# In-degrees by scans over sorted runs, rows scaled by ScalarE, plain one-hots in the first pass of a graph kernel

## The chip, the cores and the metric

The kernel runs on one core of a Trainium2 chip. Its time is the device time of one launch in microseconds (us); lower is better. The kernel before has been timed in three runs, and one more execution was recorded by the profiler. All numbers of busy time and of single instructions come from that one profiled execution.

## The reference, cut to what matters

A graph of 6250 nodes with 256 features and 106,250 edges (source, target, weight). The edges are sorted by target: `dst = dst[argsort(dst)]`, and every node has at least its self-loop. Four graph layers follow one another, with a layer norm after each. Only the first has something to do with the change:

```python
deg_out = segment_sum(edge_weight, src, num_segments=N)
deg_in  = segment_sum(edge_weight, dst, num_segments=N)
norm    = edge_weight * rsqrt(deg_out[src] * deg_in[dst] + EPS)
# one layer: xt = x @ W ; agg = segment_sum(xt[src] * norm[:, None], dst) ; relu(agg + b)
```

This layer is applied twice with the same edges and norms (the first and the second pass below). A later layer divides by the number of edges that end in a node (the counts), and the last one sums over the edges in both directions.

## The kernel before, in words

The nodes are cut into 49 blocks of 128. The edges are laid out so that each *tile* of 128 edges has its targets in one block; the first pass has 888 tiles (`T`), later passes 880. A tile's messages are summed in three steps. GpSimd (POOL) gathers the 128 source rows from a table in HBM into a slot of a ring (one indirect DMA of 128 x 257 numbers: 256 features, and in column 257 the source's out-degree). TensorE (PE) multiplies the rows with a one-hot matrix, edge by node of the block, into one of four PSUM banks. VectorE (DVE) adds the bank to the block's sums in SBUF (`acc`).

**Preamble.** Edges are loaded as 128 partitions of 840 (`J`) edges, sorted. DVE plans the layout by target (`plan_by_dst`, `place_blocks`, L1646 to L1649). Edge records of three words (source, target, weight) go to HBM (L614), and POOL reads windows of them back (`windows`), which PE turns so that each tile is a column (`turn_windows`): `d_idx` (source row), `d_loc` (node of the block), `d_norm` (at first the weight). Out-degrees are sums of products of one-hots (`out_degrees`, DVE L1671 to L1674, PE L791), in chunks between the other steps. PE transposes the layers' weights (L825 to L835) behind the first chunks. Then come the in-degrees: in 74 batches of 12 tiles DVE makes bf16 one-hots of `d_loc` (L1682) and PE multiplies them with the weights split into three bf16 parts and a column of ones (L800), two tables of sums per tile are reduced (L1690, L1691) and summed by block on PE (L813). Meanwhile POOL waits for the out-degrees, which SyncE (SP) writes into the table (L406, L408), and then fills the ring of 40 slots (L660), ahead of the pass. `l0_ready` starts the pass on PE and ScalarE (ACT).

**First pass.** All engines run loops of 40 tiles (a *turn*: five *octets* of 8 tiles): 17 turns in which DVE also places ranks for a later pass, 5 without, and one last octet. The order of DVE is written out by hand in `scatter_turn`: for tile u it does the extras of `next_norms` or `with_places`, makes the one-hot of tile u times the norm (L1871, one scalar instruction: equal, then multiply), and adds tile u - 2 (L1860). The extras compute the norms of the next octet. SP loads the octet's target numbers, broadcast to all partitions (L418, 256 KB); at u = 0 of an octet DVE compares them with the node numbers (`row_onehots`, L1919); PE multiplies the result with the table of in-degrees (`degrees_of`, L917, eight bf16 matmuls) to give the in-degree of each edge; at u = 4 DVE reduces three parts (L1925) and multiplies with column 257 of the gathered rows (L1931); ACT takes the root (L1275); at u = 6 DVE inverts it (L1936) and multiplies it into `d_norm` (L1938). PE's loop is `first_pass` (L934, a matmul of 256 columns per tile). POOL's is `first_gathers`, which waits until the matmul that last read a slot is done. ACT also turns the gather's indices into integers for the next turn (L1271). At u = 2, 18, 34 of the first 17 turns DVE places one block of source ranks (`place_of_block`): compare 840 edges with the block (L1721), scan them (L1722), copy where the mask is set (L1724).

After the pass a dense stage, the second pass (its tables are read at L630) and the three further layers follow. The change doesn't touch them.

Of the kernel before, what the change touches and what calls it, by code (L numbers as in the profile page):

```python
# [99 lines left out]
def build(nc, A, out):  # L100
# [26 lines left out]
    ROW_BUF = (0, 1, 2, 0, 1)  # L127
# [17 lines left out]
    with ctx:  # L145
# [9 lines left out]
        numbers = bank[6][:, 0:P]  # L155

# [33 lines left out]
        parts_d = acc_flat[:, 10240:10240 + 2 * TC].bitcast(BF16).rearrange("p (t w) -> p t w", w=4)  # L190
        loc_k = acc_flat[:, 0:TC].bitcast(BF16).rearrange("p (t r) -> p t r", r=2)
# [30 lines left out]
        def part(n, dt=F32):  # L222
# [14 lines left out]
        mask = part(J // 2, BF16)  # L237
# [3 lines left out]
        ROWS = RING * P  # L241
        loc_rows, row_oh = (big[:, at_dst + o:at_dst + o + 3 * ROWS // 2].bitcast(BF16).rearrange("p (v n) -> p v n", v=3)
                            for o in (0, 3 * ROWS // 2))
        assert 3 * ROWS <= 7 * J // 2 + 2 * J
# [8 lines left out]
        w_sums, c_sums = s_idx[:, :], s_loc[:, :]  # L253
        loc_w = ring[:, TG * 512:TG * 512 + TG * P // 2].bitcast(BF16).rearrange("p (g n) -> p g n", g=TG)
# [9 lines left out]
        turned_sums = oh[:, 0:7, :].rearrange("p r n -> p (r n)")  # L264
# [59 lines left out]
        waited pool_waited act_waited first_staged totals_ready listed signs codes win_free acc_clear sums_ready sums_t sums_c sums_done sort_low sort_high sort_mm sort_out places table_in degrees locs_out locs_ready di_oh di_mm di_z root  # L324
        s_ready dego_mm dego_oh loc_ready prefix_done flag_ready win_d_ready diag_ready
        blk_bcast slow_pos rec_d_done win_d_in win_turned deg_oh
        deg_mm
# [38 lines left out]
        def _(sp):  # L366
# [35 lines left out]
            sp.wait_ge(S["locs_ready"], 1)  # L402
            sp.dma_start(loc_dram.rearrange("(g p n) -> p g n", p=P, n=P), loc_w).then_inc(S["locs_out"], 16)
# [5 lines left out]

            sp.wait_ge(S["locs_out"], 16)  # L410
            sp.wait_ge(S["codes"], 1)

            def load_rows(i, v, since):

                if since is not None:
                    sp.wait_ge(S["di_oh"], i * WIDE + (v - since + 1))
                b = ROW_BUF[v]
                sp.dma_start(loc_rows[:, b, :], loc_dram[ds(i * (WIDE * ROWS) + v * ROWS, ROWS)].partition_broadcast(P)).then_inc(rows_in[b], 16)  # L418

# [783 lines left out]
        def _(act):  # L1203
# [55 lines left out]
            for k, first in ((0, 0), (1, 3)):  # L1259
                if k:  # L1260
                    act.wait_ge(S["sums_done"], 1)
# [1198 lines left out]
```

## Time and profile before

| | us |
|---|---|
| median of three runs | 8519.04 (8510.78 to 8534.96) |
| profiled execution, its own time | 8506.99 |
| its span, first to last instruction | 8505.2 |
| busy in the span: PE / DVE / ACT / POOL | 5829.8 / 4220.0 / 1769.0 / 4359.4 |
| preamble (first one-hot of the pass at 401) | about 400 |
| last add of the first pass | 1813 |

Read the table so: the busy times overlap, and a share over the whole span says little about one stage. The preamble and the first pass are together 1813 us of 8505; DVE was busy in them 1203 us, POOL 912 us, PE 1090 us and ACT 161 us. The mean granted clock of PE over the span was 0.704 of full speed (2.4 GHz); in the first pass the windows of 200 us show 0.63 to 0.69.

### The profile page before, as it was taken

What the parts mean: (1) busy time and instruction counts of PE and PEld (TensorE: products, weight loads), DVE (VectorE), ACT (ScalarE), POOL (GpSimd) and SP (SyncE); (2) the same over time, 40 slices, a digit from 0 to 9 for tenths busy, and PEclk for the clock granted to TensorE, in tenths of its full rate; (3) what the DMA queues carried; (4) which work ended last, traced back from release to release, by engine and by line L of the source; (5) the groups of instructions that cost most, each with busy time, mean ns of one, the idle gap of its engine ahead of it and who ended that gap; (6) DMA issues with size and microseconds to landing.
All of it is one profiled execution on the core that took longest, in us unless ns stands there. A gap on an engine that the chain in (4) does not pass through costs nothing. (4 is left out here: it accounts for less than half of the span.)

```text
span 8505.2 us, 118243 instructions
## 1 busy us (share of the span) xinstructions
PE 5829.8 (69%) x23570; PEld 3830.4 (45%) x23571; DVE 4220.0 (50%) x10149; ACT 1769.0 (21%) x3207; POOL 4359.4 (51%) x4466
## 2 busy tenths in 40 slices
PE   5466666678888887996666666797666666666564
PEld 4333333345555555674454444454333333333332
DVE  8766666545555555884555555565222222222224
ACT  4100000015666663122222222253000000000000
POOL 0266666626666665004555555302666666666664
PEclk7566666689999998767878887897555555555555
DMA  2133333333222221232222222411221113111112
GB/s 81 41 103 99 100 99 100 106 91 102 81 81 82 81 81 50 78 131 87 72 72 73 73 72 72 95 33 42 56 56 50 45 45 45 45 45 46 44 45 63
DMA packets 309340, 609.28 MB, mean 72 GB/s; under 512 B 89530, under 2 KB 163590, under 8 KB 309064
## 3 DMA queue, kind: packets, MB, share of 16 engines
q0 software_dynamic: 184128, 466.71, 20.4%
q1 hardware_dynamic: 125064, 141.13, 5.5%
q14 instruction: 121, 0.99, 0.0%
q8 instruction: 27, 0.44, 0.0%
HBM read 563.79 MB, written 50.13 MB: 72 GB/s over the span
## 5 line engine op out<-in xcount | busy, mean ns | idle before, releaser
L895 PE MATMUL bank<-ring,oh 128*128 128x128 f32 x3520 | 1350.3, 495 | 960.3 <-DMA ring<-fwd_table,stage_i 465.4
L895 PEld LDWEIGHTS bank<-ring,oh 128*128 128x128 f32 x3520 | 876.1, 312 | 1556.2 <-issue 1552.2
L630 POOL DMA_INDIRECT ring<-h_table,stage_i x880 | 877.2, 997 | 658.4 <-issue 326.3
L1860 DVE TENSOR_TENSOR acc<-bank,acc 128x256 f32 x1768 | 749.9, 424 | 797.4 <-PE bank L974 389.7
L630 POOL DMA_INDIRECT ring<-fwd_table,stage_i x880 | 832.1, 946 | 508.5 <-issue 267.6
L630 POOL DMA_INDIRECT ring<-bwd_table,stage_i x880 | 832.4, 946 | 448.4 <-PE bank L895 221.5
L1321 ACT ACTIVATE ring<-big 128x889 f16<-128x889 f16 x840 | 831.3, 1032 | 539.0 <-PE bank L985 335.8
L985 PE MATMUL bank<-ring,big 128*128 128x445 f16 (+1 forms) x3360 | 826.6, 370 | 146.6 <-ACT ring L1321 123.2
L1110 PE MATMUL bank<-big,oht 128*128 x2640 | 457.1, 340 | 481.8 <-ACT oht L1436 461.9
L660 POOL DMA_INDIRECT big<-x_and_degree,stage_i x536 | 533.2, 995 | 447.5 <-PE bank L934 286.2
L934 PE MATMUL bank<-big,oh 128*128 128x256 f32 x1072 | 507.3, 620 | 356.5 <-DVE oh L1871 278.5
L1902 DVE TENSOR_TENSOR acc<-bank,acc 128x1024 f32 x220 | 269.3, 1224 | 920.0 <-PE bank L895 757.9
L1871 DVE TENSOR_SCALAR oh<-iota,d_loc,d_norm 128x128 f32<-128x128 f32 x1768 | 632.4, 361 | 102.5 <-issue 34.6
L974 PE MATMUL bank<-ring,oh 128*128 128x256 f32 x1760 | 576.1, 412 | 125.2 <-DVE oh L1871 92.0
L985 PEld LDWEIGHTS bank<-ring,big 128*128 128x128 f16 x3360 | 478.5, 146 | 379.1 <-ACT ring L1321 161.3
L1110 PEld LDWEIGHTS bank<-big,oht 128*128 128x128 bf16 x2640 | 306.2, 116 | 624.1 <-issue 531.3
L1126 PE MATMUL bank<-ring,oh 128*128 128x257 f32 x1760 | 529.0, 435 | 5.8 <-issue 2.0
L934 PEld LDWEIGHTS bank<-big,oh 128*128 128x128 f32 x1072 | 269.8, 290 | 557.4 <-DVE oh L1871 329.2
L717 POOL DMA_INDIRECT ring<-q_table,stage_i x296 | 281.3, 950 | 356.0 <-issue 209.7
L2247 DVE TENSOR_TENSOR acc<-bank,acc 128x257 f32 x880 | 373.6, 424 | 167.4 <-DVE acc L2247 68.5
L974 PEld LDWEIGHTS bank<-ring,oh 128*128 128x128 f32 x1760 | 345.4, 204 | 229.7 <-issue 99.0
L660 POOL DMA_INDIRECT ring<-x_and_degree,stage_i x352 | 355.9, 1011 | 165.2 <-issue 89.6
(443 smaller groups left out, 7899.5 us busy)
## 6 DMA issues: line engine op xcount, KB each, us to landing
big<-places_in_block SPq DMA_DIRECT2D x111, 256.0 KB
acc<-places_in_block SPq DMA_DIRECT2D x74, 384.0 KB
ring<-h_table,stage_i POOLq DMA_INDIRECT x880
ring<-fwd_table,stage_i POOLq DMA_INDIRECT x880
ring<-bwd_table,stage_i POOLq DMA_INDIRECT x880
big<-x_and_degree,stage_i POOLq DMA_INDIRECT x536
h_table<-hq SPq DMA_DIRECT2D x50, 128.0 KB, 1.7
x_table<-ring SPq DMA_DIRECT2D x25, 256.0 KB, 2.1
```

Of the source, the lines that this page charges most:

```text
L630: pool.indirect_dma_start(out=gbuf[:, u % RING, 0:width], out_offset=None, in_=table, in_offset=bass.IndirectOffsetOnAxis(ap=stage_i[:, v, ...
L660: pool.indirect_dma_start(out=first_bufs[v][:, r, 0:D + 1], out_offset=None, in_=xd_dram, in_offset=bass.IndirectOffsetOnAxis(ap=stage_i[: ...
L895: pe.matmul(sums[:, ds(b, 1), :].rearrange("p b f -> p (b f)"), oh[:, place, :], gbuf[:, u, 0:P], start=False, stop=True, skip_group_check ...
L934: pe.matmul(bank[u % 4][:, 0:D], oh[:, u % 4, :], first_bufs[v][:, r, 0:D], start=True, stop=True).then_inc(S["mm"], 1)
L974: pe.matmul(bank[u % 4][:, 0:D], oh[:, u % 4, :], gbuf[:, r, 0:D], start=True, stop=True).then_inc(S["mm"], 1)
L985: mm = pe.matmul(bank[4 + 2 * k + h][:, 0:hi - lo], low_k[2 * w + k][:, :, r:r + 1].rearrange("p n a -> p (n a)"), high_k[(u + 2 * RING) % ...
L1110: mm = pe.matmul(bank[2 + u // 2][:, u % 2 * D:(u % 2 + 1) * D], oht[:, h % 2, u * P:(u + 1) * P], p3[:, s, ds(b, 1), :].rearrange("p a f ...
L1126: pe.matmul(bank[4 + u][:, 0:D + 1], oh[:, t % 12, :], msg[:, t % RING, :], start=True, stop=True).then_inc(S["l2_c"], 1)
L1321: act.activation(high_k[u % 3], iota_h, ACT.Sign, bias=high_bias[:, ds(j, 1)]).then_inc(S["sort_high"], 1)
L1860: dve.tensor_tensor(to, bank[u % 4][:, 0:width], to, ALU.add).then_inc(S["accd"], 1)
L1871: o = dve.tensor_scalar(oh[:, u % 4, :], iota[:, :], loc[:, t], weight[:, t], ALU.is_equal, ALU.mult)
L2247: dve.tensor_tensor(to, bank[4 + u][:, 0:D + 1], to, ALU.add).then_inc(S["l2_acc"], 1)
```

## The change

1. `in_degrees`, `tile_weights`, `sums_by_block`, `degrees_of`, `row_onehots`, SP's `load_rows`, the one-hots of tiles (L1715) and the split of weights (L1754 to L1757) go. In their place `run_sums` computes the in-degree of each edge in the order of the records: as the edges are sorted by target, each node is a run. A scan forward sums within a run, a scan backward spreads the run's last value over it; since a run can cross partitions, PE turns the partitions' ends into a row (`join_runs`), a small scan joins them, and the big scan is repeated with the carry. The in-degree becomes a fourth word of the records, and arrives by the windows in `deg_slot`, laid out like the norms.
2. In the first pass DVE makes plain one-hots, four tiles in one instruction, from numbers kept in PSUM. ACT multiplies the eight gathered rows of an octet with their norms in place (`scaled_rows`), and PE waits for that once an octet. Column 257 is set to one after the product of the degrees is taken, so that the matmul and the add of 257 columns also count the edges; `cnt_in` is copied out at the end.
3. The scan of the rank placement writes to PSUM, and its unused second operand is a PSUM number.
4. Codes, totals, the repeated iota and the bias split, which stood between the in-degree batches, stand in a row before `l0_ready`. `acc` is cleared by POOL alone.

```diff
+            def join_runs():
+                ends = (scan_out[:, J - 1:J], run_dst[:, 0:1], run_dst[:, J - 1:J])
+                pe.wait_ge(S["run_rows"], 1)
+                for k, end in enumerate(ends):
+                    mm = pe.matmul(bank[2][0:1, k * P:(k + 1) * P], end, ident[:, :], start=True, stop=True)
...
             broadcast_blocks(0, 2)
+            join_runs()
             pe.wait_ge(S["weights_in"], 16 * len(NAT))
...
-            turn_windows(3, S["win_d_in"])
+            turn_windows(4, S["win_d_in"])
...
+            def run_sums():
+                at = lambda k, n=P: run_row[:, k:k + n]
+                carry = cols[:, 15:16]
+                dve.wait_ge(S["records_sorted"], 1)
+                link(dve.memset(same[:, 0:1], 1.0))
+                link(dve.tensor_tensor(same[:, 1:J], run_dst[:, 1:J], run_dst[:, 0:J - 1], ALU.is_equal))
+                link(dve.tensor_tensor_scan(scan_out, mask, run_w, 0.0, ALU.mult, ALU.add))
+                dve.sem_inc(S["run_rows"], 1)
...
+                link(dve.tensor_tensor_scan(at(2 * P), at(5 * P + 1), at(P), 0.0, ALU.mult, ALU.add))
...
+                link(dve.tensor_tensor_scan(scan_out, mask, run_w, carry, ALU.mult, ALU.add))
+                link(dve.scalar_tensor_tensor(pos_f, same[:, 1:J + 1], 0.0, scan_out, ALU.is_equal, ALU.mult))
+                link(dve.tensor_tensor_scan(scan_out[:, ::-1], same[:, 1:J + 1][:, ::-1], pos_f[:, ::-1], 0.0, ALU.mult, ALU.add))
...
+                link(dve.tensor_tensor_scan(run_deg[:, ::-1], same[:, 1:J + 1][:, ::-1], pos_f[:, ::-1], carry, ALU.mult, ALU.add))
+                dve.sem_inc(S["runs_ready"], 1)
...
+            def scaled_rows(i, v):
+                act.wait_ge(S["norms"], i * WIDE + v + 1)
+                for r in range(RING):
+                    row = first_bufs[v][:, r, 0:D]
+                    o = act.activation(row, row, ACT.Copy, scale=d_norm[:, ds(i * LONG + v * RING + r, 1)])
+                o.then_inc(S["scaled"], 1)
...
             def roots_and_places(i, octets):
                 for v in range(WIDE):
                     roots(i, v)
+                    scaled_rows(i, v)
                     if v < octets:
                         stage(d_idx, i * LONG + LONG + v * RING, v)
...
-            def place_of_block(b, kb, base):
+            def place_of_block(b, kb, base, rank, other):
                 link(dve.tensor_scalar(mask, kb, iota[:, ds(b, 1)], None, ALU.is_equal))
-                link(dve.tensor_tensor_scan(scan_out, mask, mask, base[:, ds(b, 1)], ALU.add, ALU.bypass))
+                link(dve.tensor_tensor_scan(rank, mask, other, base[:, ds(b, 1)], ALU.add, ALU.bypass))
                 apart(dve, S["waited"])
-                link(dve.copy_predicated(pos_f, mask.bitcast(I16), scan_out))
+                link(dve.copy_predicated(pos_f, mask.bitcast(I16), rank))
...
             def edge_norms(i, v):
                 dve.wait_ge(S["root"], i * WIDE + v + 1)
+                dve.memset(last_column(v), 1.0)
                 link(dve.reciprocal(z8[:, v, :], z8[:, v, :]))
                 norms = d_norm[:, ds(i * LONG + v * RING, RING)]
                 link(dve.tensor_tensor(norms, norms, z8[:, v, :], ALU.mult))
+                dve.sem_inc(S["norms"], 1)
...
+                def four_one_hots(i, h):
+                    place = h % 2 * GROUP
+                    dve.wait_ge(S["mm"], i * LONG + h * GROUP + 8 - GROUP)
+                    dve.tensor_tensor(oh[:, place:place + GROUP, :], first_numbers.unsqueeze(1).to_broadcast([P, GROUP, P]),
+                                      d_loc[:, ds(i * LONG + h * GROUP, GROUP)].unsqueeze(2).to_broadcast([P, GROUP, P]), ALU.is_equal).then_inc(S["one_hot"], GROUP)
...
+                def turn(i, groups, last, places):
+                    for h in range(groups):
+                        v, at = (h // 2 + 1) % WIDE, i + (h // 2 + 1) // WIDE
+                        if not last:
+                            (edge_norms if h % 2 else degree_products)(at, v)
+                        if not last or h + 1 < groups:
+                            four_one_hots(i, h + 1)
+                        for u in range(h * GROUP, (h + 1) * GROUP):
+                            add(i, u)
+                            if places and u in (2, 18, 34):
+                                place_of_block(i * 3 + u // 16, src_kb, sm["base_s"], ranks, unused.to_broadcast([P, J]))
```

## Rows read from the trace of the kernel before

**Rows 1.** Busy us (instructions) by engine, clock, DMA share, GB/s; 200 us
```profile
600.00:800.00 200.00, 125.36 (x372) 71.92 (x371) 130.00 (x343) 5.99 (x30) 122.00 (x121) 0.64 0.38 100
```

**Rows 2.** Groups by line: DVE, first pass; count, busy us, mean ns, idle before
```profile
L1860 DVE TENSOR_TENSOR acc<-bank,acc 128x256 f32 x888 | 376.6, 424 | 230.0 <-issue 144.3 <-PE bank L934 62.2 <-remote 16.5
L1871 DVE TENSOR_SCALAR oh<-iota,d_loc,d_norm 128x128 f32<-128x128 f32 x888 | 320.9, 364 | 58.6 <-issue 23.0 <-DVE acc L1860 7.7 <-DVE big L1724 4.3
L1722 DVE TENSOR_TENSOR_SCAN big<-big,base_s 128x840 f32<-128x840 bf16 x51 | 100.3, 1968 | 6.3
L1919 DVE TENSOR_SCALAR big<-big,node_no 128x1024 bf16<-128x1024 bf16 x111 | 56.0, 504 | 46.6 <-issue 45.9 <-DVE d_norm L1938 0.2
L1724 DVE COPY_PREDICATED big<-big 128x840 f32<-128x840 int16 x51 | 55.8, 1095 | 7.7 <-issue 5.8 <-DVE big L1722 2.0
L1721 DVE TENSOR_SCALAR big<-big,iota 128x840 bf16<-128x840 bf16 x51 | 23.0, 451 | 0.0
...
L1925 DVE TENSOR_REDUCE z<-bank 128x8 f32<-128x24 f32 x111 | 19.6, 176 | 141.5 <-remote 138.2 <-PE bank L917 2.2 <-PE bank L934 1.0
```

**Rows 3.** Waits of DVE, 1580 to 1765 us: total us, times, longest
```profile
DVE z L1925 <- remote: 53.6, 14, 5.2
```

**Rows 4.** Timeline of DVE: start us, duration us, instruction, idle before and releaser
```profile
1659.22 0.18 DVE L1925 TENSOR_REDUCE z<-bank 128x8 f32<-128x24 f32 x1 [5.07 <-remote]
```

**Rows 5.** Timeline of PE around the same wait (each tile is two matmuls)
```profile
1652.97 1.07 PE L917 MATMUL bank<-table,big 128*128 x8
...
1659.97 5.71 PE L934 MATMUL bank<-ring,oh 128*128 128x256 f32 x12 [4.78 <-DVE oh L1871]
```

**Rows 6.** Timeline of POOL: first and 40th gather; gathers at 821 to 828
```profile
276.11 1.69 POOL L660 DMA_INDIRECT big<-x_and_degree,stage_i  x1 [0.84 <-POOL stage_i L642]
...
333.25 0.95 POOL L660 DMA_INDIRECT big<-x_and_degree,stage_i  x1 [0.30 <-issue]
...
821.41 2.05 POOL L660 DMA_INDIRECT ring<-x_and_degree,stage_i  x1 [0.30 <-issue]
...
826.29 0.95 POOL L660 DMA_INDIRECT ring<-x_and_degree,stage_i  x1 [0.31 <-issue]
827.54 0.95 POOL L660 DMA_INDIRECT ring<-x_and_degree,stage_i  x1 [0.30 <-issue]
```

**Rows 7.** Timeline of DVE in the preamble
```profile
84.73 1.95 DVE L1715 TENSOR_SCALAR tile_oh<-iota,blk_c 128x49 f32<-128x49 f32 x7 [0.16 <-DVE win_i_d L1624]
...
91.41 0.69 DVE L1648 CAST blk_d<-bank 128x512 int32<-128x512 f32 x1 [0.89 <-PE bank L769]
...
113.53 0.47 DVE L1671 TENSOR_TENSOR big<-iota_b,s_loc 128x600 bf16<-128x600 bf16 x1 [13.88 <-PE bank L791]
...
219.83 2.53 DVE L1748 TENSOR_SCALAR ring<-ring,blk_c 128x128 bf16<-128x128 f32 x7
...
231.73 2.15 DVE L1587 TENSOR_TENSOR acc<-ring,acc 128x896 bf16<-128x896 f32 x1
...
262.87 0.45 DVE L1765 TENSOR_TENSOR deg_out<-bank,deg_out 128x49 f32<-128x49 f32 x2
...
338.33 7.91 DVE L1682 TENSOR_TENSOR big<-iota_b,acc 128x1536 bf16<-128x1536 bf16 x9 [13.79 <-remote]
...
394.06 2.23 DVE L2054 MEMSET acc<- 128x2610 f32 x1 [0.61 <-DVE acc L2053]
...
400.97 0.60 DVE L1871 TENSOR_SCALAR oh<-iota,d_loc,d_norm 128x128 f32<-128x128 f32 x2
```

**Rows 8.** Timeline of ACT in a later stage: PSUM to SBUF, bias by pointer
```profile
3342.30 0.47 ACT L1356 ACTIVATE ring<-bank,cols 128x256 f32<-128x256 f32 x1
3342.66 0.48 ACT L1357 ACTIVATE ring<-bank,cols 128x256 f32<-128x256 f32 x1
```

**Rows 9.** Timeline of DVE in the third pass: adds of 257 columns
```profile
4301.98 0.43 DVE L2247 TENSOR_TENSOR acc<-bank,acc 128x257 f32 x1 [0.21 <-DVE acc L2247]
```

**Rows 10.** Groups by line, whole span: four one-hots in one instruction
```profile
L1882 DVE TENSOR_TENSOR oh<-bank,d_loc 128x512 f32<-128x512 f32 x220 | 150.7, 687 | 491.3 <-PE bank L895 442.3 <-remote 29.9 <-issue 18.9
```

More of the change, by code:

```diff
@@ L155, in build @@
         numbers = bank[6][:, 0:P]
+        first_numbers = bank[4][:, 0:P]
+        ranks, unused = psum[:, 6 * 512:6 * 512 + J], bank[7][:, 511:512]
         NX = NBE * D
@@ L323, in build @@
         names = """consts pads_set edges_in weights_in wt_turned wt_copied wt_stored dve_chain pe_chain
[L324 to L327, printed above, removed]
+        waited pool_waited act_waited first_staged totals_ready listed signs codes win_free acc_clear records_sorted runs_ready records_out run_rows run_cols sort_low sort_high sort_mm sort_out places table_in degrees locs_out di_z root norms scaled
+        s_ready dego_mm dego_oh prefix_done flag_ready win_d_ready diag_ready
+        blk_bcast slow_pos rec_d_done win_d_in win_turned
         x2_rest gru_rows values_ready slot_val slot_cp slot_prod slot_acc slot_eq slot_sel slot_w_ready pool_chain h_sum l0_ready staged one_hot mm accd d_staged
@@ L408, in _ @@
             sp.dma_start(xd_dram[(NB - 1) * P:N, D:D + 1], deg_out[0:LAST, NB - 1:NB], allow_slow_non_contiguous=True).then_inc(S["table_in"], 16)
[L410 to L418, printed above, removed]
-            for v in range(WIDE):
-                load_rows(0, v, (None, None, None, 3, 3)[v])
-            with sp.Fori(1, LONG_TURNS) as i:
-                for v in range(WIDE):
-                    load_rows(i, v, (2, 2, 5, 3, 3)[v])
-            load_rows(LONG_TURNS, 0, 2)
             def store_h6(i, q):
@@ L924, in first_pass @@
                     n = i * LONG + u
-                    if r == 2 and not last:
-                        degrees_of(i + (v + 1) // WIDE, (v + 1) % WIDE)
-                    pe.wait_ge(S["one_hot"], n + 1)
-                    if v == 0:
-                        pe.wait_ge(gd[r], i * 16 + 16)
-                    elif r == 0:
-                        pe.wait_ge(octet_in[v], i * (16 * RING) + 16 * RING)
+                    if u % GROUP == 0:
+                        pe.wait_ge(S["one_hot"], n + GROUP)
+                    if r == 0:
+                        pe.wait_ge(S["scaled"], i * WIDE + v + 1)
                     pe.wait_ge(S["accd"], n + 1)
-                    pe.matmul(bank[u % 4][:, 0:D], oh[:, u % 4, :], first_bufs[v][:, r, 0:D], start=True, stop=True).then_inc(S["mm"], 1)
+                    pe.matmul(bank[u % 4][:, 0:D + 1], oh[:, r, :], first_bufs[v][:, r, 0:D + 1], start=True, stop=True).then_inc(S["mm"], 1)
             pe.wait_ge(S["l0_ready"], 1)
-            degrees_of(0, 0)
             with pe.Fori(0, LONG_TURNS) as i:
@@ L1798, in _ @@
+            link(dve.tensor_scalar(val_lo, pos_f, 1.0, None, ALU.add))
+            dve.sem_inc(S["codes"], 1)
+            totals(1, signs_s, sm["tot_s"])
+            link(dve.tensor_copy(iota_k, iota_b[:, :].unsqueeze(2).to_broadcast([P, P, BATCH])))
             plan_by_src()
             link(dve.memset(pos_f, float((TC - 1) * P)))
-            dve.wait_ge(S["sums_done"], 1)
-            link(dve.tensor_copy(sm["deg_in"][:, 0:NB], bank[2][:, 0:NB]))
-            dve.sem_inc(S["degrees"], 1)
```

225 lines of the change are left out of this document (84 added, 141 removed).

## The prediction

> **What bounds the kernel now.** The busy shares were read first, then the windows of the first pass, then its groups by line, waits and timeline. No engine is full over the span, and the chain of waits names nothing but its last instruction, so the stage that the diff touches must be read by itself. It is the preamble (0 to 396 us) and the first pass, whose adds run from about 401 to 1813 us: 1412 us for 888 tiles, 1.59 us a tile, 63.6 us a turn of 40. In 200 us of it [rows 1] DVE works 130 us, POOL 122 and PE 125; no one of the three is full.
>
> DVE's sum [rows 2]: per tile an add (424 ns) and a one-hot (364 ns); per octet 504 + 176 + 172 + 192 + 167 ns of degree work; and 51 rank placements of 451 + 1968 + 1095 ns = 3.51 us. Of its idle time 141.5 us stand before L1925, the first instruction that reads what L917's matmuls wrote. Where no placements run, that wait comes once an octet, 14 times in 185 us, up to 5.2 us [rows 3]. The timeline shows its form: L917's eight matmuls end at 1654.0 [rows 5], the reduction that needs them starts at 1659.22 after 5.07 us idle, released "remote" [rows 4], and PE's next tiles start at 1659.97 because DVE's one-hots stood behind it [rows 5]. The result was computed 5 us before DVE was told. The preamble has the same late news: L1682 waits 13.79 us at 338.33 for the small matmuls of L800, while gathers stream [rows 7]. So DVE, which holds one-hots and adds together, sets the pace: its own work of about 48 us plus stalls of 12 to 16 us a turn.
>
> POOL's floor: gathers back to back stand 1.25 us apart (826.29, 827.54), and one took 2.05 us at 821.41, beside a rank scan [rows 6]. 40 gathers are 50 us against the 63.6 of a turn.
>
> **The change, part by part.** (1) *Preamble, run sums.* Added on DVE behind the plan: four scans of 840 at 1.97 us [rows 2] = 7.9; two full-width operations at about 1.1 (taken from L1724's 1.095 [rows 2]) = 2.2; 16 small ones of 0.1 to 0.3, 4 in all; four round trips to PE at 0.9 (the wait before 91.41 [rows 7]) and three 128-column transposes, 5. About 20 us, and 16 to 25 by leaving out or doubling the small terms. It takes the place of L1715 (1.95 [rows 7]). PE's weight transposes now stand behind the third reply, so the stall of DVE's out-degree loop that ends at 113.53 with 13.88 us [rows 7] moves back nearly whole: +20. The records go to HBM after it, and the windows are read by POOL in that shadow. A fourth record word adds a third to PE's turning of windows (21 transposes, 4.7 us, for which DVE waits): +1.6. From the block between 219.83 and 233.88 [rows 7] only the cast, the d_loc update and the maximum remain, 2.4 us of 14.9: -12.5. Out-degrees, ready at 263.3 [rows 7], come at 263.3 + 20 + 1.6 - 12.5 = 272.4; I take 274. The first gather, 276.11 before [rows 6], starts at about 287, and the first octet has landed by about 304.
>
> (2) *Preamble, in-degree one-hots.* All 74 batches of L1682/L800 with their waits go, and the two reductions by block, which end at 386.2. What stood between them stays (sums over the same timeline; hidden, so their rows are not shown): codes 4.3, totals 0.7, the repeated iota 1.0, the source plan 4.6, a fill 0.9, place_blocks 5.7, bias split 6. That is 23 us: l0_ready at 274 + 24 = 298, hidden behind the first gathers. The two fills before the pass (3 us, the second at 394.06 [rows 7]) are POOL's now, hidden under its long wait. The first tile then needs the product, the root, the norms and eight scaled rows, 4.3 us: 308.5 against the one-hots at 400.97 [rows 7], with the matmul at 401.5. **93 us earlier.** The cover matters: 40 gathers from 287 end near 345 (57 us before, 276.11 to 333.25 [rows 6]), so POOL is at work at the start and no longer 69 us ahead.
>
> (3) *DVE in the pass.* Gone per octet: 504 + 176 ns, and L917 with its late news; per four tiles 4 x 364 ns of one-hots become one of 687 ns [rows 10]. That looks like a gain and is none: adds alone stand 0.43 + 0.21 = 0.64 us apart, each waiting for the one before [rows 9], and a one-hot of 0.36 fills that gap (the pair takes the same 0.64), while the 0.687 of four fill no gap. DVE's own work is per octet 8 x 0.64 + 2 x 0.687 + 0.17 + 0.4 + 0.1 = 7.2 us, or 36 a turn, plus three placements at 3.51 = 46.5: about what it was (per octet 5.1 + 1.2 = 6.3 plus gaps). What goes is the stall of 12 to 16 us a turn, with L917.
>
> (4) *ScalarE scales rows.* No row shows 128x257 in SBUF with a scale pointer. Nearest: 128x256 with a pointer, 0.47 long, 0.36 apart [rows 8]. Eight rows, 8 x 0.36 + 0.1 = 3.0 us; ends 2.0 (the pace of half the width) and 4.5 (0.56 apart). It is on the path: PE can't start an octet until all eight are done, and the norms come in the middle of the octet before. From there 0.7 + 3.0 = 3.7 us run against PE's four remaining tiles, at 0.95 each (six in 5.71 us [rows 5]) 3.8 us, and the add lags its tile by 0.6. So an octet takes 7.6 + 0.7 = 8.3 us, 41.5 a turn; of three placements (3.51 + 0.3 of waits each) between nothing and all is in series, 41.5 to 53.
>
> (5) *POOL* waits for slots that PE has read, 40 tiles back. With PE no longer stopped 12 to 16 us a turn, what is late next is POOL itself: 40 x 1.25 = 50. A scan in PSUM may or may not hold gathers; if it does, three times 1.1 us. POOL at 50 to 53, PE and ACT at 41.5 to 53, DVE at 46.5: three near-equal loops through one ring make more than the largest. I take POOL's floor and 2 us of lost handovers, 55 with placements (50 + 3.3 + 2) and 52 without, since POOL's row is the one measured at full pace: 17 x 55 + 5 x 52 + 12 for the last octet and the first start = 1207. Ends: 1118 (gathers back to back, below) and 1412 (no gain).
>
> The Trainium skill ("SBUF — State Buffer", "Who interferes with whom") says that a DVE instruction with two SBUF inputs contends with a GpSimd one that reads SBUF, and one with a single SBUF input doesn't. The gather of 2.05 us fits it; by it the PSUM scan gives POOL 17 x 3.3 = 56 us if POOL is what bounds, and the sum would go from 1207 to 1151; copy_predicated still reads two SBUF operands.
>
> (6) A 257th column: adds of 128x257 take 0.43, as 256 [rows 2, 9]; nothing. The rest of the kernel is as it was.
>
> Sum: pass from 308.5 to 1516 instead of 401.5 to 1813: 93 + 204 = 297 us. The profiled execution, 8506.99 (span 8505.2 and 1.8 around it), becomes 8210. The median of the runs, 8519.04, lies 12 above it, so **8222 us**.
>
> **Rivals.** *POOL back to back.* For: after the ring fills there is no reason to wait but the free slot, and the scan may stop holding gathers. Against: PE and ACT's loop is as long. 287 + 57 + 848 x 1.25 + 12 = 1416, saving 397: 8122.
>
> *The pass keeps its pace.* If the late news hangs on streaming gathers and not on L917, whatever replaces it (the norms, `scaled`) inherits it: one late reply per octet as before, 64 a turn. Only the preamble is gained: 8519 - 93 = 8426. Against: L934's own updates aren't late unless they stand behind L917.
>
> *Slower: the scaling chain in series.* DVE's product, ACT's root, DVE's norms, eight ACT rows and PE's start are five handovers. If ACT's rows take 4.5, PE gets its octet only after them (the norms reach ACT late, behind placements), and each octet also has 1 us of handovers: 0.7 + 4.5 + 1 + 7.6 = 13.8 us, plus 10.5 of placements a turn: 17 x 79.5 + 5 x 69 + 14 = 1710, against 1412: +298 - 93 = +205, or 8724; with rows at 3.0 it is 12.3 an octet, 1545, +40, or 8559. It turns at (1412 + 93)/111 = 13.56 us per octet, placements in it.
>
> *It doesn't do what it says*: PSUM scans still hold gathers and copy_predicated in PSUM takes longer; 17 x 3 x 1 = 51 us less gain, 8273, inside the range.
>
> **Chances.** Forecast (with the last case) 0.62, POOL back to back 0.13, pace kept 0.14, series chain 0.08, a wash between the last two 0.03. The range goes to 8118 and 8430, which takes in the two rivals that are faster than before; the likeliest's own is 8150 to 8290. Below 0.3% (25 us, about what a measurement tells from none) is the same: faster 0.89, same 0.03, slower 0.08.
>
> **What would show it.** Right: the first L934 near 308; no wait over 2 us before DVE's product; POOL's gathers 1.25 to 1.35 apart over the pass; eight ACT copies in about 3 us; last add near 1516; later stages moved by the same amount, not changed. Wrong: POOL idle 20 us a turn "<-PE", PE idle before each octet on ACT's rows, or run sums past 25 us.

## The result, and the profile after

The changed kernel takes 8534.57 us (median of 20 runs, 8522.05 to 8552.0), the kernel before 8514.51 (20 runs beside it): a ratio of 1.0022, interval 1.0014 to 1.003. It moved by less than 0.3%, where 8222 was forecast. The profiled execution took 8536.18 (span 8534.4), 29.2 more than the 8506.99 of before. By stage: PE's first tile came at 320.0 instead of 401.5 (-81.5), the first pass took 1512 us instead of 1412 (+100), the rest 6702 instead of 6692 (+11). The preamble gained what was forecast but for 12 us; the pass, forecast at 1207, lost.

The preamble of after, VectorE (start, length, engine, line, operation, count, idle time before it and what ended it): run sums, the out-degree loop behind them, the first octet's degrees.

```profile
91.28 0.06 DVE L1643 MEMSET big<- 128x1 bf16 x1 [1.31 <-DVEq L1720]
91.37 1.63 DVE L1644 TENSOR_TENSOR big<-big 128x839 bf16<-128x839 f32 x1
96.53 0.55 DVE L1648 COPY acc<-bank 1x384 f32<-1x384 f32 x1 [1.59 <-PE bank L779]
...
108.62 1.97 DVE L1672 TENSOR_TENSOR_SCAN big<-big,cols 128x840 f32<-128x840 bf16 x1
...
127.94 0.47 DVE L1630 TENSOR_TENSOR big<-iota_b,s_loc 128x600 bf16<-128x600 bf16 x1 [11.58 <-PE bank L771]
...
291.79 0.17 DVE L1875 TENSOR_TENSOR z<-big 128x8 f32<-128x8 f32 x1 [0.54 <-DVE bias_parts L1683]
...
316.01 0.19 DVE L1881 RECIPROCAL z<-z 128x8 f32<-128x8 f32 x1 [23.42 <-issue]
```

Run sums end at 110.6, 19.3 us after they could begin. The degrees' product is done at 292.0, but the reciprocal comes only at 316.01. ScalarE's rows at that place tell why:

```profile
314.28 1.28 ACT L1241 ACT_TABLE_LOAD   x1 [66.50 <-POOL stage_i L623]
315.57 0.20 ACT L1241 ACTIVATE cols<-half_less 128x1 f32<-128x1 f32 x1
315.68 0.28 ACT L1224 ACTIVATE z<-z,cols 128x8 f32<-128x8 f32 x1
316.60 3.30 ACT L1231 ACTIVATE big<-big,d_norm 128x256 f32<-128x256 f32 x8 [0.63 <-issue]
```

ACT's stream begins with a wait until POOL has staged the indices of all five octets (`first_staged`, L623), and POOL stages the fifth after some 28 gathers. It stands in before too, where nothing needed ACT so early.

The first pass. In the window from 600 to 800 us (busy time and count of each engine, granted clock of PE, DMA share, GB/s), to be held against [rows 1]:

```profile
600.00:800.00 200.00, 91.52 (x219) 56.38 (x220) 101.87 (x223) 50.78 (x140) 105.53 (x112) 0.64 0.28 75
```

PE, DVE and POOL all do less than before: POOL gathers for 112 tiles instead of 121. The groups (busy, mean ns | idle before, releaser) that answer to [rows 2], and the waits from 500 to 1500 us (total, times, longest):

```profile
L1904 DVE TENSOR_TENSOR acc<-bank,acc 128x257 f32 x888 | 377.0, 425 | 610.7 <-issue 320.1 <-PE bank L891 146.5 <-remote 64.3
L1892 DVE TENSOR_TENSOR oh<-bank,d_loc 128x512 f32<-128x512 f32 x220 | 151.6, 689 | 45.5 <-issue 23.3 <-DVE d_norm L1883 18.5 <-PE bank L891 2.1
L1701 DVE TENSOR_TENSOR_SCAN bank<-big,base_s,bank 128x840 f32<-128x840 bf16 x51 | 100.6, 1972 | 21.3 <-PE bank L891 7.7 <-issue 6.6 <-DVE big L1700 3.0
```

```profile
PEld bank L891 <- DVE acc L1904: 453.7, 145, 7.1
ACT big L1231 <- DVEq L1884: 433.1, 34, 17.7
POOL big L641 <- PE bank L891: 215.6, 143, 4.4
...
DVE acc L1904 <- issue: 194.2, 129, 5.8
```

The instructions cost what was taken. DVE is idle 610.7 us before the adds, mostly "issue": time in which it waited for nothing that the profile shows. A timeline of 17 us shows what that is. DVE first, then POOL in the same time:

```profile
999.74 0.43 DVE L1904 TENSOR_TENSOR acc<-bank,acc 128x257 f32 x1 [3.19 <-issue]
1003.29 0.42 DVE L1904 TENSOR_TENSOR acc<-bank,acc 128x257 f32 x1 [3.13 <-issue]
...
1010.68 0.41 DVE L1904 TENSOR_TENSOR acc<-bank,acc 128x257 f32 x1
1011.31 0.42 DVE L1904 TENSOR_TENSOR acc<-bank,acc 128x257 f32 x1 [0.21 <-DVE acc L1904]
1011.95 0.43 DVE L1904 TENSOR_TENSOR acc<-bank,acc 128x257 f32 x1 [0.21 <-DVE acc L1904]
```

```profile
999.55 0.94 POOL L641 DMA_INDIRECT ring<-x_and_degree,stage_i  x1 [0.30 <-issue]
1000.80 0.95 POOL L641 DMA_INDIRECT ring<-x_and_degree,stage_i  x1 [0.30 <-issue]
1002.05 0.95 POOL L641 DMA_INDIRECT ring<-x_and_degree,stage_i  x1 [0.30 <-issue]
1005.39 0.94 POOL L641 DMA_INDIRECT ring<-x_and_degree,stage_i  x1 [2.39 <-issue]
```

Until 1002.05 POOL gathers without a break, 1.25 us apart, and adds stand 3.5 us apart. POOL pauses 2.4 us at 1003, and soon after the adds stand 0.64 apart. The trace's records of DVE's register and semaphore instructions, which the views leave out, say the rest: in such a stretch most of them take 0.69 to 0.73 us instead of 0.02 to 0.06, also those that wait for nothing, or the next one starts 0.7 us later. PE only follows: its next tile starts at 1000.22, 0.05 us after the add of 999.74 ends, while the next add comes 3.5 us after that one. ScalarE's and POOL's own such records stay at 0.02 to 0.05 us, so what is slow itself is DVE. I call these **slow stretches**. In after all 44 streaks of 11 to 13 gathers (gaps under 0.4 us) have one, and 8 of the 152 shorter ones hold two or more such records; the first comes 5.7 to 7.9 us after the streak begins, the last ends at most 3.1 us after the streak's end. Before has them too: in all 15 streaks of 14 to 16 gathers, but only 13.2 to 15.3 us after their start, and in 18 of its 69 streaks of 4 to 8. And a streak alone isn't enough: POOL fills the ring of after in one of 47 gathers from 278.8 on, DVE's records stay short until 292.5, when it goes idle, and again from 316 to 323, and the first long one comes at 324.6, when the pass runs. Adds of before in a slow stretch:

```profile
703.65 0.43 DVE L1860 TENSOR_TENSOR acc<-bank,acc 128x256 f32 x1 [3.09 <-issue]
705.06 0.35 DVE L1871 TENSOR_SCALAR oh<-iota,d_loc,d_norm 128x128 f32<-128x128 f32 x1 [0.99 <-issue]
707.37 0.42 DVE L1860 TENSOR_TENSOR acc<-bank,acc 128x256 f32 x1 [1.96 <-PE bank L934]
```

A turn of 40 tiles with placements, from add to add, takes 71.1 us (69.6 to 72.0; the first, behind the filling of the ring, 86.1) against 65.5 before (64.8 to 68.2). It holds two streaks of 11 to 13 gathers; before it held one of about 15 and shorter ones.

One thing is needed to read what follows: the experiments ran on three chips, on which the same kernel before takes 7070, 8426 and 8511 to 8516 us, so each is compared with before on its own chip. (Where a run has no interval, it was timed once.)

### The profile page after: what moved, and what is told of

It reads as the page before. It is cut to its first block and busy times, and to the rows that moved or that the text cites. A ratio compares the mean times of both kernels' runs of the same rounds, so it can differ in the third digit from the quotient of the medians.

```text
span 8534.4 us, 112153 instructions
## 1 busy us (share of the span) xinstructions
PE 5613.5 (66%) x21773; PEld 3736.3 (44%) x21774; DVE 3984.8 (47%) x9278; ACT 2129.1 (25%) x4093; POOL 4311.8 (51%) x4466
## 5 line engine op out<-in xcount | busy, mean ns | idle before, releaser
L865 PEld LDWEIGHTS bank<-ring,oh 128*128 128x128 f32 x3520 | 876.8, 312 | 1560.7 <-issue 1555.8
L891 PE MATMUL bank<-big,oh 128*128 128x257 f32 x1072 | 448.1, 574 | 511.8 <-DVE acc L1904 192.7
L641 POOL DMA_INDIRECT big<-x_and_degree,stage_i x536 | 508.0, 948 | 426.4 <-PE bank L891 282.0
L1904 DVE TENSOR_TENSOR acc<-bank,acc 128x257 f32 x888 | 377.0, 425 | 610.7 <-issue 320.1
L1810 DVE TENSOR_TENSOR acc<-bank,acc 128x256 f32 x880 | 373.2, 424 | 565.7 <-PE bank L930 380.6
L1082 PE MATMUL bank<-ring,oh 128*128 128x257 f32 x1760 | 533.8, 438 | 8.2 <-issue 3.3
L891 PE MATMUL bank<-ring,oh 128*128 128x257 f32 x704 | 277.6, 550 | 310.1 <-DVE acc L1904 150.1
L641 POOL DMA_INDIRECT ring<-x_and_degree,stage_i x352 | 333.6, 948 | 248.3 <-PE bank L891 149.3
L2211 DVE TENSOR_TENSOR acc<-bank,acc 128x257 f32 x880 | 373.4, 424 | 168.5 <-issue 71.0
```

The costliest lines, as they stand in the source:

```text
L641: pool.indirect_dma_start(out=first_bufs[v][:, r, 0:D + 1], out_offset=None, in_=xd_dram, in_offset=bass.IndirectOffsetOnAxis(ap=stage_i[: ...
L865: pe.matmul(sums[:, ds(b, 1), :].rearrange("p b f -> p (b f)"), oh[:, place, :], gbuf[:, u, 0:P], start=False, stop=True, skip_group_check ...
L891: pe.matmul(bank[u % 4][:, 0:D + 1], oh[:, r, :], first_bufs[v][:, r, 0:D + 1], start=True, stop=True).then_inc(S["mm"], 1)
L1082: pe.matmul(bank[4 + u][:, 0:D + 1], oh[:, t % 12, :], msg[:, t % RING, :], start=True, stop=True).then_inc(S["l2_c"], 1)
L1810: dve.tensor_tensor(to, bank[u % 4][:, 0:width], to, ALU.add).then_inc(S["accd"], 1)
L1904: dve.tensor_tensor(to, bank[u % 4][:, 0:D + 1], to, ALU.add).then_inc(S["accd"], 1)
```

## The experiments

Theory: what costs is the slow stretches, brought by long streaks of gathers, whoever consumes them. Rivals: ACT's scaling chain in series; the rank scan in PSUM; the bytes of the gathers; and, for the start, ACT's wait. In the diffs "..." marks lines or arguments left out.

**Set 1: reads as pauses, and ACT's wait.** Three register reads on POOL before each octet of gathers (`after_oct3`); one before the first and the fifth (`after_half`); the three on the kernel before (`before_oct3`).

```diff
+                    if not first and r in (0,):
+                        for _ in range(3):
+                            pool.load([idle_reg], flag_i[0:1, 0:1])
...
                     pool.indirect_dma_start(out=first_bufs[v][:, r, 0:D + 1], ...
```

> The changed kernel; POOL reads a register from SBUF three times before the first gather of every octet of the loop (about 2 us), so that at most 8 gathers stand back to back. Theory A (a streak of 11 or more back-to-back gathers makes every instruction of the sequencers take 0.7 us): the slow stretches of about 10 us, two in each turn with placements, go; the turn falls from 71 us to what POOL's 40 gathers and 5 pauses take, 59 to 62, and the time from 8535 to 8340 to 8400. Theory B (the stalls hang on the place in the code or on PE's late news, not on POOL's streaks): the stretches stay, POOL has 9 us more in each turn, and the time is 8535 to 8650.

> The changed kernel; one such register read before the first and the fifth gather of every octet (streaks of 4, gaps of 0.9 us). Theory A: as with one long pause an octet, turn 59 to 62, time 8340 to 8400, no slow stretches. If it takes a long gap to end a streak, stretches remain and the time is 8450 to 8550. Theory B: 8535 to 8650.

> The kernel before, with the same three register reads before the first gather of every octet. Theory A: its slow stretches (one of 8 to 10 us in most turns, and the waits before the reduction of degrees in turns without placements) go too; the turn falls from 66 to 59 to 61, the time from 8515 to 8390 to 8430. Theory B: 8515 to 8620.

Measured beside 7069.72 for before (one run each): 7029.15, 7030.39 and 7065.70. The edit made no pause: the gathers stayed 1.25 us apart. The trace holds no record of the reads, so where they went isn't shown. The gathers of `after_oct3`:

```profile
699.34 0.95 POOL L645 DMA_INDIRECT big<-x_and_degree,stage_i  x1 [0.30 <-issue]
700.59 0.95 POOL L645 DMA_INDIRECT big<-x_and_degree,stage_i  x1 [0.30 <-PE bank L895]
```

But this chip showed more than was asked. It has no slow stretches, with streaks of 39 gathers and more, and the kernel before is 1445 us faster on it, 270 of them in the first pass; the rest of the kernel gains too.

ACT stages each octet's indices only when POOL has staged them, not all five before anything else:

```diff
-            act.wait_ge(S["first_staged"], WIDE)
...
                     scaled_rows(i, v)
                     if v < octets:
+                        act.wait_ge(S["first_staged"], v + 1)
                         stage(d_idx, i * LONG + LONG + v * RING, v)
```

> The changed kernel; ACT waits for POOL's staging of the first 40 tiles not before the first root but before it overwrites each octet's indices. Both theories: the first product's root is taken near 292 instead of 315.7 us, the first matmul of the pass comes at 297 to 300 instead of 320, and the time falls by 10 to 20 us (8515 to 8525), less if the ring is then empty sooner.

Measured: 7012.38, 17 less than `after_oct3` and 57 less than before. The windows of `before_oct3`, then of `after_act`, without slow stretches:

```profile
600.00:800.00 200.00, 137.39 (x440) 77.17 (x440) 156.41 (x425) 7.20 (x36) 154.41 (x150) 0.72 0.45 124
```

```profile
600.00:800.00 200.00, 107.06 (x290) 73.36 (x290) 129.70 (x290) 65.64 (x181) 141.94 (x151) 0.70 0.37 99
```

150 gathers in 200 us against 151. The median turn with placements takes 53.4 us in the old form and 54.7 in the new, and the pass, from PE's first tile to the last add, 1142 (369.7 to 1511.9) and 1159 (297.6 to 1456.5). So where nothing is slow, the change gains the preamble alone: the old loop takes 53.4 us a turn once its late news is gone, and the new one no less. POOL's gathers say what bounds each. In `before_oct3` they stand in one streak of 724: 40 x 1.25 is 50, three gathers a turn take 2.05 us beside a rank scan, and that makes 53.3; turns of POOL without placements take 50.0. In `after_act` no gather takes over 1.2 us, but from the seventh turn on POOL waits twice near the head of each turn, some 5 us, for tiles that PE has not done: there PE's and DVE's loop binds, not POOL. The clock granted is higher here too (0.70 against 0.64), but that isn't the difference: outside slow stretches adds stand 0.64 us apart in after as here, and the idle time before the adds of `after_act`, 260.9 us against 610.7 in after, has no "issue" among its three largest parts:

```profile
L1903 DVE TENSOR_TENSOR acc<-bank,acc 128x257 f32 x888 | 377.4, 425 | 260.9 <-PE bank L891 145.1 <-DVE acc L1903 89.2 <-DVE big L1702 16.3
```

**Set 2: parts undone.** The change as it is, in three rounds (`after_same`); DVE multiplies the one-hots by the norm again and ACT scales nothing (`dve_scale`, which leaves out the counts); the rank scan back in SBUF (`scan_sbuf`).

```diff
-                    scaled_rows(i, v)
...
-                    if u % GROUP == 0:
-                        pe.wait_ge(S["one_hot"], n + GROUP)
-                    if r == 0:
-                        pe.wait_ge(S["scaled"], i * WIDE + v + 1)
+                    pe.wait_ge(S["one_hot"], n + 1)
```

```diff
-                        place_of_block(..., src_kb, sm["base_s"], ranks, unused.to_broadcast([P, J]))
+                        place_of_block(..., src_kb, sm["base_s"], scan_out, mask)
```

> The changed kernel, nothing altered. The last four kernels ran where the kernel before takes 7070 us instead of 8515, with no stretch of slow instructions. Theory C (the slow stretches belong to where a kernel is run and hit both kernels; without them the pass of both is a loop of about 54 us a turn): the preamble's gain of 75 to 81 us (first matmul at 320 instead of 401, or 396 without stalls) shows, the pass costs 5 to 15 more, and the time is 0.990 to 0.997 of before. Where the slow stretches are present: 1.002 of before, as in the pair on record. If the first theory (streaks of gathers) held everywhere, the ratio would be 1.00 here too.

> The changed kernel without ScalarE's scaling: DVE makes each tile's one-hot times norm as before and PE waits for it per tile; the column of ones is then summed with norms in place of ones, so the counts are left out. Theory C1 (handing the norms to ScalarE and waiting for eight rows costs the pass about 4 us a turn, 53.7 to 54.7 against a DVE loop that has lost L1919 and L1925): turns with placements 49.5 to 51.5 us, POOL's floor of 50, and 60 to 90 us less than the changed kernel. C2 (the turn is set by POOL and by the branch, not by scaling): within 20 us of the changed kernel.

> The changed kernel with the rank scan's operands back in SBUF. If the scan in SBUF holds gathers (2.05 us instead of 0.95 beside one) and POOL bounds: 51 times 1.1 = up to 56 us slower. If DVE, ACT and PE's loop bounds the turns with placements (54.4 against POOL's 50 to 53), within 15 us of the changed kernel.

Measured beside 8426.2: `after_same` 8441.98 (ratio 1.002, 1.001 to 1.0029), `dve_scale` 8431.59, `scan_sbuf` 8442.93. Turns with placements: 68.3 to 70.4, 67.6 to 68.8, 67.5 to 70.4. Slow stretches stand in all three: in each of the 44 streaks of 11 or more gathers that each of them has. Taking ACT's chain out of the loop gives back about 1 us a turn (68.2 for 69.3 in the median), where some 15 are missing against the 54.7 of `after_act`, so that chain is not the loss. With the scan in SBUF a gather takes longer, and here, where POOL waits for PE anyway, the time is the same (`scan_sbuf`, groups of POOL in the pass; 948 ns in after):

```profile
L641 POOL DMA_INDIRECT big<-x_and_degree,stage_i x518 | 514.7, 994 | 389.9 <-PE bank L891 236.4 <-issue 121.0 <-remote 32.5
L641 POOL DMA_INDIRECT ring<-x_and_degree,stage_i x336 | 330.1, 982 | 207.4 <-PE bank L891 96.7 <-issue 71.1 <-remote 39.6
```

**Set 3: real pauses.** POOL itself fills 128x512 three times in a chain before each octet's first gather (`gap_octet`, from the second turn on), so that no streak is longer than eight; one fill of 128x128 before every gather (`gap_each`); the three fills on the kernel before (`gap_before`); ACT's wait alone (`after_act2`, the edit of `after_act`).

```diff
+                    if not first and r in (0,):
...
+                        for m in range(3):
+                            pool.wait_ge(S["pool_gap"], at + m)
...
+                            pool.memset(oh[:, 8:12, :]..., 0.0).then_inc(S["pool_gap"], 1)
...
                     pool.indirect_dma_start(out=first_bufs[v][:, r, 0:D + 1], ...
```

> The changed kernel; before the first gather of every octet of the loop POOL itself executes three linked fills of 128x512 (about 2 us), so that no streak of back-to-back gathers is longer than 8. The register reads of the earlier runs ran ahead of the gathers on the sequencer and left streaks of 39. Theory A (where the kernel before takes 8400 to 8500 us, a streak of 11 or more gathers makes each instruction of the sequencers take 0.7 us): no slow stretch, turns with placements 58 to 62 us instead of 69 to 71, and 120 to 200 us less than the changed kernel (8440 beside 8426 of before). Theory B (the stretches don't hang on streaks): they stay, with 0 to 100 us more than the changed kernel. Where the kernel before takes 7070: no slow stretches anyway, POOL's floor is 60 a turn, and the time is 7110 to 7160 by both.

> The changed kernel; one fill of 128x128 on POOL before every gather of the loop, so that none is back to back (1.7 to 1.8 us from start to start instead of 1.25). Theory A: no slow stretch, the turn is POOL's 68 to 72 us, about the changed kernel's time. If only the length of a streak counts and a small gap does not end it, stretches stay and the turn is 75 or more. Where before takes 7070: 68 to 72 a turn, 7350 to 7450.

> The kernel before with the same three fills at the start of each octet. Theory A: its turns fall from 65 us to 58 to 62, 80 to 130 us less than before. Theory B: 0 to 100 us more. Where before takes 7070: 7150 to 7200.

> Again the changed kernel in which ACT's wait for POOL's staging stands before it overwrites the indices. With slow stretches: first matmul near 298, 15 to 22 us less than the changed kernel, ratio to before 0.999 to 1.001. Without them: 0.992 as in the first look.

Measured beside 8510.9: `gap_octet` 8370.44, `gap_each` 8489.21, `gap_before` 8501.82, `after_act2` 8526.74 (1.0019, 1.0008 to 1.0029). More work on POOL makes the kernel faster: `gap_octet` takes 140 us less than before beside it and 164 less than the 8534.57 of after. POOL in `gap_octet`, then its window from 600 to 1400 us beside that of after:

```profile
1001.52 0.55 POOL L645 MEMSET oh<- 128x512 f32 x1
1002.22 0.53 POOL L645 MEMSET oh<- 128x512 f32 x1 [0.15 <-issue]
1002.90 0.53 POOL L645 MEMSET oh<- 128x512 f32 x1 [0.15 <-issue]
1003.59 0.95 POOL L647 DMA_INDIRECT big<-x_and_degree,stage_i  x1 [0.17 <-issue]
```

```profile
600.00:1400.00 800.00, 405.83 (x1024) 261.75 (x1024) 454.11 (x1008) 231.04 (x637) 586.89 (x702) 0.67 0.31 84
```

```profile
600.00:1400.00 800.00, 365.86 (x892) 228.22 (x893) 399.46 (x884) 203.10 (x559) 423.72 (x448) 0.65 0.28 74
```

PE does 1024 matmuls, or 512 tiles, where it did 892, or 446 (POOL's 702 count its fills too); turns take 61.6 to 63.6 instead of 71.1, and the last add comes at 1675.0 instead of 1831.6. The stretches are shorter, not gone: two to three slow register or semaphore instructions per streak of eight, where none was expected, and the turns are longer than the 58 to 62 of the forecast. A small fill before each gather makes them start 1.33 us apart where nothing else holds them; that keeps the stretches, and turns of 65 to 70. On the kernel before the fills give 9 us, within its spread, where 80 to 130 were expected: its streaks were mostly short already, but with the fills 59 of its 106 streaks of 4 to 8 still have slow stretches. `after_act2`, expected at 0.999 to 1.001, shows the other error apart. Its PE and ACT:

```profile
297.73 3.79 PE L891 MATMUL bank<-big,oh 128*128 128x257 f32 x8 [13.62 <-issue]
```

```profile
291.97 1.28 ACT L1240 ACT_TABLE_LOAD   x1 [43.57 <-DVEq L1758]
```

The first tile comes 22 us earlier, where the forecast had l0_ready, but the first turn takes 101.5 us instead of 86.1: POOL is still filling the ring in one long streak, and DVE now meets it. On the chip without slow stretches the same turn takes 54.7.

**Set 4: both edits, and what of a streak counts.** Both (`act_gap`); the fills again (`gap_octet2`); one fill before the first and fifth gather, streaks of four with pauses of 0.7 us (`gap_half`); gathers of 16 numbers a row instead of 257 from the second turn on (`narrow`, which leaves out the features and the out-degree there).

```diff
-                    pool.indirect_dma_start(out=first_bufs[v][:, r, 0:D + 1], ...
+                    pool.indirect_dma_start(out=first_bufs[v][:, r, 0:wide], ...   # 257 in the first turn, then 16
```

> The changed kernel with both edits: ACT's wait for the staging moved, and three fills on POOL (2 us) before each octet of gathers. Theory A (streaks of gathers bring the slow stretches; gaps shorten them): where before takes 8400 to 8520, ratio to before 0.978 to 0.984 (8370 of 8511 with the gaps alone, and 8 to 20 us for the wait). Where before takes 7070, POOL's floor of 60 us a turn decides: 1.000 to 1.008.

> The changed kernel with the gaps alone again, now timed in rounds. With slow stretches: ratio 0.980 to 0.987. Without them: 1.003 to 1.010.

> The changed kernel with one fill of 0.7 us on POOL before the first and the fifth gather of each octet. Theory A with a backlog (it is the mean rate over some ten gathers that brings the stretch): mean 1.42 us a gather instead of 1.5, so stretches between those of the changed kernel and those with the long gaps: 8380 to 8450 beside 8511. If the length of a streak counts (4 here), no stretch and 8340 to 8370.

> The changed kernel; from the second turn on the gathers fetch 16 numbers a row instead of 257 (the features and the out-degree are left out, the product takes the in-degree twice). As many instructions, semaphores and DMA descriptors, a sixteenth of the bytes. If bytes on the DMA engines bring the slow stretches, they go: turns of 54 to 56 us, 220 to 260 us less than the changed kernel. If the number of gathers and their completions brings them, they stay: within 60 us of the changed kernel.

Measured beside 8515.87: `act_gap` 8379.29 (0.9846, 0.9829 to 0.9864), `gap_octet2` 8386.75 (0.9856, 0.9839 to 0.9874), `gap_half` 8516.66, `narrow` 8520.49. Both edits together beat the kernel before by 1.5%, the fills alone by 1.4%; what the moved wait adds to the fills isn't separated (the intervals overlap). The windows of `gap_half` and of `narrow`:

```profile
600.00:1400.00 800.00, 379.26 (x918) 238.55 (x916) 416.51 (x912) 210.21 (x575) 494.97 (x570) 0.64 0.28 76
```

```profile
600.00:1400.00 800.00, 369.91 (x906) 229.00 (x907) 407.26 (x903) 207.05 (x570) 429.62 (x455) 0.66 0.05 5
```

`narrow` moves 5 GB/s where after moves 74, its DMA share is 0.05, and it is as slow: turns of 69.3 to 70.8, and adds that wait. Not the bytes, then; what is left is how fast gathers follow one another, and what comes with each (descriptors, semaphore updates, their records), which no run separates. A row of `narrow`:

```profile
1022.75 0.43 DVE L1906 TENSOR_TENSOR acc<-bank,acc 128x257 f32 x1 [5.67 <-remote]
```

`gap_half` missed. No streak of it is longer than four, and its trace has more slow records of DVE (458) than that of after (329), so the length of a streak isn't what counts. By pace the runs fall into line: where nothing else holds POOL, the mean time from gather to gather is 1.25 us in after, 1.33 in `gap_each` and 1.35 in `gap_half` (a pause of 0.7 us after four), all with slow stretches and turns of 65 to 72, and 1.47 in `gap_octet` (a pause of 2.06 us after eight), with 258 slow records and turns of 62 to 64. Four values on one kernel are too few for a threshold, and the 0.4 us above only sort the streaks of these traces.

## Why the prediction was wrong

By its steps, in its order. The one that failed is (3): it charged the stall of a turn to L917 and took it off with L917.

(1) *Run sums*: right. 19.3 us for the forecast 20; the four waits for PE 1.59, 1.16, 0.74 and 0.73 for 0.9 each. The stall that was to move "back nearly whole" moved by 14.4 (127.94 for 113.53), and the first gather came at 278.75, not 287: 8 better.

(2) *First tile*: 320.0 for 308.5. DVE was ready at 291.8, 6 before the forecast; the step left out ACT's wait for `first_staged`. `after_act2` shows this: with the wait moved, 297.7. It also forecast that "the cover matters", and it was POOL's staging behind its gathers that was late.

(3) *DVE in the pass*: this step failed. "What goes is the stall of 12 to 16 us a turn, with L917." L917 went and the stall did not. The late news was never a property of L917: [rows 3 to 5] show the wait once an octet "5 us before DVE was told", and the same rows fit an L917 that merely is the matmul for which DVE waits closely while everything is slow. L1682's wait of 13.79 while gathers stream [rows 7] was read as "the same late news" and then not used: there was no L917 there. Nor did L917's share fit: [rows 2] have 141.5 us of idle time before L1925, or 6.4 a turn, and not the 12 to 16 of all stalls. The chip without slow stretches settles it. There the same two instructions of the same kernel (`before_oct3`, whose lines are numbered 4 higher) hardly wait, L1929 3.9 us in all for L1925's 141.5, and L1686 0.6 for the 29.1 of L1682 in before:

```profile
L1929 DVE TENSOR_REDUCE z<-bank 128x8 f32<-128x24 f32 x111 | 19.5, 176 | 3.9 <-PE bank L921 3.2
L1686 DVE TENSOR_TENSOR big<-iota_b,acc 128x1536 bf16<-128x1536 bf16 x74 | 65.2, 954 | 0.6 <-DVE tot_s L1597 0.2
```

```profile
L1682 DVE TENSOR_TENSOR big<-iota_b,acc 128x1536 bf16<-128x1536 bf16 x74 | 65.4, 951 | 29.1 <-remote 24.1 <-issue 3.5 <-PE bank L800 1.0
```

The measured price of the slow stretches per turn is 65.5 - 53.4 = 12.1 us in the old kernel, which the step had right in size, and 71.1 - 54.7 = 16.4 in the new, where 0 was put (the subtrahends from the chip without slow stretches, whose granted clock is higher too, so these are upper bounds). Over the pass it is 1512 - 1159 = 353 us, against 1412 - 1142 = 270 before; the forecast had 1207.

(4) *ScalarE*: eight rows in 3.30 us for 3.0, right, the handover too. On the chip without slow stretches the turn of 54.7 is what (3) to (5) put at 55, and the pass of 1159 what they put at 1207 (the turns without placements took 38 to 51.4, not 52), so the sum came out, in part by luck: it was POOL's floor of 50 with 3.3 for held gathers and 2 for handovers, and in `after_act` no gather was held and POOL waited some 5 us a turn for PE. What it was compared with was wrong: without stalls the old loop, one-hots hidden in the gaps of the adds, runs at 53.4, which is the floor of 50 + 3.3 that step (5) put on the new one. So even where the forecast's condition holds the pass gains nothing (1142 and 1159); the 204 us were set against stalls that this change had no hold on.

(5) *POOL*: PSUM scans do let gathers go (0.94 beside a scan of 1.97, as at 1005.39, against 2.05 in [rows 6]); by this the Trainium skill ("SBUF — State Buffer", "Who interferes with whom") agrees with the trace. It is worth nothing here, since POOL was not what bound: `scan_sbuf` takes the same time where there are slow stretches, and without them it wasn't tried. That copy_predicated "still reads two SBUF operands" doesn't fit the change: of its two inputs the ranks are in PSUM now, and it took 1.09 us as before. The lower end of the pass, 1118, should have been 1107 by the forecast's own rival (1416 - 308.5).

(6) *The column of ones*: 425 ns for 424, nothing, right.

Of the rivals the one that kept the pace, 8426 at 0.14, had the mechanism ("if the late news hangs on streaming gathers and not on L917, whatever replaces it inherits it"), but not that it grows, from 65.5 to 71.1 us a turn. Why it grows isn't shown. The new kernel gathers in two streaks of 11 to 13 a turn where the old one had one of about 15, and they turn slow earlier; that PE takes an octet in one go isn't the reason, since `dve_scale` waits tile by tile and has 44 such streaks too. The chain in series was not what happened: `dve_scale` has no such chain and takes 8431.59 for 8441.98, still more than before beside it. Between 8430 and 8559 the forecast had only "a wash" at 0.03, without a mechanism of its own, and that is where the time fell.

What stays open is what in the chip makes DVE's register and semaphore instructions slow. What the runs exclude as its cause is bytes, the scan, ACT's work and L917. One sign stands in the traces. A gather adds 16 to its semaphore, and in `after_oct3` and `before_oct3`, without slow stretches, there are 16 records of that for each gather; in before and after, and in `narrow` as well, there are about five (from 370 to 1470 us). So where the stretches are, the trace is incomplete (42,217 semaphore updates in after, 100,896 in `after_act`), and "remote" before a wait, as in [rows 3 and 4], can stand for a releaser whose record is missing. The Trainium skill ("NOTIFIC — the notification-queue block", "Overflow: three behaviours, one of which stalls the engine") describes a path of records that can hold the engine that produces them when it fills; no run here shows whether that is at work. It is a rival of its own kind, since then the recording, and not the kernel, would make the stretches: every timed run here comes with a recorded span and granted clock, and an experiment that isolates it wasn't made.

## What to carry to other kernels

Before a stall is priced by the instruction that ends it, look at what surrounds it: if unrelated instructions near it also start late "by issue", the stall belongs to the stretch and outlives the instruction. Ask of the old loop what it would take without its stalls; here that was 53.4 us, and it capped the gain. Where gathers at full pace make DVE slow, a pause of about 2 us in POOL before every eighth gather was worth 1.4% against the kernel before (`gap_octet2`), and shorter pauses, at 1.33 and 1.35 us a gather, gave 0.3% and nothing, in one run each. Whether a chip has such stretches is worth a look first: the same kernel took 7070, 8426 and 8511 us on three. And a wait at the head of an engine's stream is read again whenever that engine gets a role earlier than before.

## What the hardware showed that was not expected

- While POOL gathers 1.25 to 1.35 us apart and the other engines work, DVE's register and semaphore instructions take about 0.7 us instead of 0.02 to 0.06 (5.7 to 7.9 us after a streak begins in after, 13.2 to 15.3 us in the long ones of before); on one of three chips they never did, in streaks of up to 724, and the same kernel took 7070 us there instead of 8426 to 8516. Whether the recording has a part in it is open.
- Where this happens, the traces hold about 5 of a gather's 16 semaphore updates, and on the chip without it all 16.
- On the chip without it the first pass of the kernel before is bound by POOL: 40 gathers at 1.25 us, three of them at 2.05 beside a rank scan in SBUF, make its turn of 53.4; with the scan in PSUM no gather took over 1.2 us (`before_oct3`, `after_act`).
- Three register reads on POOL before an octet put no time between its gathers (1.25 us, as without).
- ACT scales 128x256 in SBUF by a column at 0.41 us an instruction (3.30 for eight).
- A comparison of 128x839 f32 operands one element apart into bf16 took 1.63 us.
